# First attention of a macaron network: scores made twice, keys on partitions the second time, mask added by TensorE

## The reference

```python
q = (x @ Wq + bq).reshape(B, S, H, hd).transpose(0, 2, 1, 3)   # B 8, S 512, H 16, hd 8
k, v = ...                                                      # the same with Wk, Wv
scores = einsum('bhqd,bhkd->bhqk', q, k) / sqrt(hd)
band = abs(idx[:, None] - idx[None, :]) <= half                 # half = w // 2, w from 24 to 120
attn = softmax(where(band, scores, -1e30), axis=-1)
out = einsum('bhqk,bhkd->bhqd', attn, v)
out = einsum('bhqd,hdk->bhqk', out, W_o)                        # then @ Wfc + bfc, added to x
```

## Time and profile before

| | |
|---|---|
| median of 3 runs | 3266.82 us (3265.24 to 3267.09) |
| the profiled execution, its own time | 3267.73 us |
| its span, first to last instruction | 3265.8 us |
| busy in the span: TensorE (PE), its weight loads (PEld) | 81%, 56% |
| VectorE (DVE), ScalarE (ACT), GpSimd (POOL) | 74%, 71%, 50% |
| mean granted TensorE clock | 0.849 of 2.4 GHz |

### The profile page before, as it was taken

The page is one execution under the profiler, slowest core; times in us unless marked ns, Lnnn a source line. Parts: engine busy times, 40 slices in busy tenths (PEclk is TensorE's granted clock), DMA queues, the critical chain, the costliest instruction groups (busy, mean ns, idle before and its releaser), DMA issues. The chain is left out here.

```text
span 3265.8 us, 44956 instructions
## 1 busy us (share of the span) xinstructions
PE 2641.5 (81%) x13816; PEld 1818.6 (56%) x13818; DVE 2432.7 (74%) x4559; ACT 2312.6 (71%) x2789; POOL 1636.1 (50%) x1225
## 2 busy tenths in 40 slices
PE   4999958888859999399996587777777877549998
PEld 3877746666648777287774232232332322248887
DVE  5677757777756777688886787877878878378887
ACT  2555547676735555377772999999999999647776
POOL 2676620000026666454443666766767576444444
PEclk9999979898979999699997667676766676679999
DMA  3111100000001111211110000000000000021111
GB/s 111 52 52 39 39 1 2 0 0 0 0 28 52 52 39 39 79 52 40 52 39 0 0 1 1 1 1 1 1 1 1 1 1 1 0 92 52 52 39 51
DMA packets 13576, 86.60 MB, mean 27 GB/s; under 512 B 2176, under 2 KB 4224, under 8 KB 4224
## 3 DMA queue, kind: packets, MB, share of 16 engines
q1 hardware_dynamic: 13440, 84.96, 7.0%
HBM read 82.33 MB, written 2.62 MB: 26 GB/s over the span
## 5 line engine op out<-in xcount | busy, mean ns | idle before, releaser
L1648 POOL TENSOR_TENSOR A_Y<-A_Y,A_U 128x2048 f32<-128x2048 f32 x86 | 390.0, 4556 | 225.4 <-ACT A_U L1691 225.4
L1724 DVE TENSOR_SCALAR A_U<-ps 128x1024 f32<-128x1024 f32 x256 | 309.3, 1218 | 123.2 <-POOL A_Y L1648 59.3
L1730 DVE SCALAR_TENSOR_TENSOR A_U<-ps,A_U 128x1024 f32<-128x1024 f32 x256 | 311.3, 1216 | 55.6 <-PE ps L1860 55.6
L1860 PE MATMUL ps<-A_QT,A_KT 9*128 9x512 f32 x512 | 182.2, 707 | 194.2 <-DVE A_U L1730 160.9
L477 POOL TENSOR_TENSOR F0b_h<-F0b_h,dn 128x512 f32<-128x512 f32 x128 | 212.4, 1663 | 123.5 <-DVE F0b_h L408 123.3
L477 POOL TENSOR_TENSOR F0a_h<-F0a_h,dn 128x512 f32<-128x512 f32 x128 | 212.5, 1664 | 116.3 <-DVE F0a_h L408 116.1
L1860 PEld LDWEIGHTS ps<-A_QT,A_KT 9*128 9x128 f32 x512 | 66.3, 255 | 331.6 <-DVE A_U L1730 241.3
L1648 POOL TENSOR_TENSOR dn<-dn,A_U 128x2048 f32<-128x2048 f32 x42 | 190.3, 4551 | 112.1 <-ACT A_U L1691 112.1
L1691 ACT ACTIVATE A_U<-A_U 128x2048 f32<-128x2048 f32 (+1 forms) x96 | 236.5, 2464 | 0.0
L1832 PE MATMUL ps<-A_Y,A_VA 128*32 128x512 f32 x688 | 227.5, 795 | 5.8 <-DVE A_OT L1630 3.0
L1088 ACT ACTIVATE A_M<-A_M,A_nmax 128x192 f32<-128x192 f32 (+1 forms) x512 | 203.8, 471 | 34.0 <-DVE A_nmax L1203 32.3
(11 more groups left out here) (365 smaller groups left out, 8350.9 us busy)
## 6 DMA issues: line engine op xcount, KB each, us to landing
dn<-weight_rows SPq DMA_DIRECT2D x32, 1024.0 KB, 4.7
F1a_cwb<-weight_rows SPq DMA_DIRECT2D x16, 1024.0 KB, 4.6
F1b_cwb<-weight_rows SPq DMA_DIRECT2D x16, 1024.0 KB, 4.7
dn<-in_down SPq DMA_DIRECT2D x2, 2048.0 KB, 12.3
stage<-in_up SPq DMA_DIRECT2D x1, 2560.0 KB, 9.1
X<-in_x SPq DMA_DIRECT2D x1, 2048.0 KB, 8.2
F1a_h<-in_up SPq DMA_DIRECT2D x1, 2048.0 KB, 7.7
F1b_h<-in_up SPq DMA_DIRECT2D x1, 2048.0 KB, 7.8
```

The lines of the kernel that those rows point to most:

```text
L1648: eng.tensor_tensor(flat(y_slot(m, h)), flat(y_slot(m, h)), flat(Um[:, h % UR]), ALU.add).then_inc(s["t_ready"], 1)
L1724: eng.tensor_scalar(u_step(n), d_pair(n), 0.0, None, ALU.max).then_inc(s["dp_vector"], 1)
L1730: eng.scalar_tensor_tensor(out=u, in0=g_pair(), scalar=CLAMP, in1=u, op0=ALU.min, op1=ALU.mult).then_inc(s["u_ready"], 1)
L1860: last = eng.matmul(ps[:, 4 + b, :], KT[r:r + 9, pair, kt * P:(kt + 1) * P], QT[r:r + 9, pair, :], start=True, stop=True)
```

## The change

It works on the same tiles in another order.

- A chunk still has 16 units, but a unit is now two **halves**: half `h` is one head and two neighbouring tiles, which share one bank (`half_of`, `half_bank`, three banks in turn). TensorE first writes the mask into the bank with a bf16 matmul by the identity (`edge_b`, 512 columns), then adds the two tiles' scores. One VectorE reduction takes the maxima of both tiles and writes them into column 24 of QA.
- The rows of q are turned a second time with these maxima in (`QM`), KA holds -1 in that place. `shifted`, seven units later (`BEHIND`), makes the scores again with keys on partitions, 25 rows, again with a mask matmul first, 448 columns: they come out less their maxima. ScalarE takes the exponential straight from PSUM to PT (`weights`). The transposes of exponentials, their copies and M are gone.
- `outputs`, eight units behind, works on 192 or 256 queries at a time, all in bank 6, and OT holds a group of four heads in place of a tile.
- q and k rows are transposed by groups of four heads (`turn`, 12 groups of four a chunk), one group in each of three of four units, all through bank 3 and copied by ScalarE (`take_turned`).
- GpSimd makes QA, KA and VA and adds the output bias; projections go through bank 7 one after the other at units 5, 6 and 7. QA, VA and OT are doubled. The chunks are written out in pairs (`all_chunks`), and the last seven units of a chunk's second scores run in the next chunk.

The heart of it:

```diff
-                    for t in range(TPC):
-                        for side, src in enumerate((QA, KA)):
-                            for g in range(4):
-                                last = eng.transpose(ps[:, bank_of(t, side), g * P:(g + 1) * P], ...)
-                def scores(n):
-                    t, u = n // 4, n % 4
-                    lo, hi, w0, w1 = window(t)
-                    for r in range(2):
-                        for b in range(2):
-                            g, j = unit_head(u, r, b)
-                            last = eng.matmul(ps[:, 2 * (n % 2) + b, r * WIN + w0:r * WIN + w1],
-                                              QT[32 * j:32 * j + 24, g, t * P:(t + 1) * P],
-                                              KT[32 * j:32 * j + 24, g, lo:hi], start=True, stop=True)
-                def turn(n):
-                    ...
-                                last = eng.transpose(ps[0:k1 - k0, 4 + k, i * P:(i + 1) * P],
-                                                     M[:, n % MR, b, r, k0:k1], ident[:, :])
+                def turn(number, src, g):
+                    eng.wait_ge(s["taken"], number)
+                    for t in range(TPC):
+                        last = eng.transpose(ps[:, TURN, t * P:(t + 1) * P],
+                            src[:, t, 4 * g:4 * g + 4, :].rearrange("p h r -> p (h r)").bitcast(F32), ident[:, :])
+                    last.then_inc(s["qk_tr"], 1)
+                def scores(c, n, first):
+                    for h in (2 * n, 2 * n + 1):
+                        g, t2, j = half_of(h)
+                        if h >= 3:
+                            eng.wait_ge(s["m_ready"], c * HALVES + h - 2)
+                        ...
+                        r = 32 * j
+                        eng.matmul(ps[:, half_bank(h), :], ident_b[:, :], edge_b[:, t2, :], start=True,
+                                   stop=False, skip_group_check=True)
+                        for t in (2 * t2, 2 * t2 + 1):
+                            lo, hi, w0, w1 = window(t)
+                            last = eng.matmul(ps[:, half_bank(h), (t % 2) * WIN + w0:(t % 2) * WIN + w1],
+                                              QT[r:r + 24, g % 2, t * P:(t + 1) * P],
+                                              KT[r:r + 24, g, lo:hi], start=False, stop=True, skip_group_check=True)
+                        last.then_inc(s["sc_done"], 1)
+                def shifted(c, u, taken=None):
+                    g, m2 = u // 4, u // 2 % 2
+                    n = UNITS * c + u
+                    a, b = span(m2)
+                    ...
+                    for i in range(2):
+                        r = 32 * (2 * (u % 2) + i)
+                        eng.wait_ge(s["exp_done"], 2 * n - 1 + i)
+                        eng.matmul(ps[:, 4 + i, a:b], ident_b[:, :], mask_b[:, a:b], start=True, stop=False, ...)
+                        for m in (2 * m2, 2 * m2 + 1):
+                            lo, hi, w0, w1 = window(m)
+                            last = eng.matmul(ps[:, 4 + i, (m % 2) * WIN + w0:(m % 2) * WIN + w1],
+                                              KT[r:r + 25, g, m * P:(m + 1) * P], QM[r:r + 25, g % 2, lo:hi],
+                                              start=False, stop=True, skip_group_check=True)
+                        last.then_inc(s["s2_done"], 1)
-                                last = eng.tensor_tensor_reduce(M[:, n % MR, b, r, w0:w1],
-                                    ps[:, 2 * (n % 2) + b, r * WIN + w0:r * WIN + w1], mask[:, w0:w1],
-                                    -1.0, 3e38, ALU.add, ALU.min, nmax[:, n % MR, b, r:r + 1])
+                            last = eng.tensor_reduce(
+                                QA[:, p, 2 * t2:2 * t2 + 2, 4 * g + j, 3 * HD:3 * HD + 1]...,
+                                ps[:, half_bank(h), :].rearrange("p (t w) -> p t w", t=2), AX.X, ALU.max)
-                                last = eng.activation(m, m, ACT.Exp, scale=-1.0, bias=nmax[:, n % MR, b, r:r + 1])
+                    for i in range(2):
+                        eng.wait_ge(s["s2_done"], 2 * n + i + 1)
+                        eng.wait_ge(s["pv_done"], pair - 1)
+                        eng.activation(PT[:, m2, 2 * (u % 2) + i, a:b], ps[:, 4 + i, a:b],
+                                       ACT.Exp).then_inc(s["exp_done"], 1)
+                            for j in range(4):
+                                last = eng.matmul(ps[32 * j:32 * j + 32, OUT0, lo:hi], VA[:, p, m, 4 * g + j, :],
+                                                  PT[:, m2, j, (m % 2) * WIN + w0:(m % 2) * WIN + w1],
+                                                  start=(m == 0), stop=(m == TPC - 1), skip_group_check=True)
```

More of the change, by code:

```diff
@@ L1051, in _ @@
+                        all_chunks(eng, chunk)
                         norm_gpsimd(eng, s, B)
@@ new lines, in _ @@
+                        all_chunks(eng, chunk)
+                        for n in range(LAST + 1):
+                            if n == 2:
+                                take_turned(2 + TURNED * B, QM[:, 1, :])
+                            if n == 3:
+                                copy_out(B - 1, 1, 2)
+                            if n < BEHIND:
+                                weights(B - 1, n + UNITS - BEHIND)
+                            if n == 2:
+                                norm_scalar(eng, s, B, B - 2, nxt, SPARE)
@@ L1225, in _ @@
[L1225 to L1234 removed]
+                        eng.drain()
@@ new lines, in _ @@
+                        for b in range(2):
+                            eng.tensor_copy(mask_b[:, b * WIN:(b + 1) * WIN], mask[:, :])
+                            for k in range(2):
+                                eng.tensor_copy(edge_b[:, k, b * WIN:(b + 1) * WIN], mask[:, :])
+                        eng.drain()
+                        eng.memset(edge_b[:, 0, 0:HALO], NEG)
+                        eng.memset(edge_b[:, 1, 2 * WIN - HALO:2 * WIN], NEG)
+                        eng.drain().then_inc(step, 1)
@@ new lines, in chunk @@
+                        def chunk(c, p, done):
+                            first = done == 0
+                            for n in range(UNITS):
+                                maxima(c, p, n)
+                                if n == 0:
+                                    norm_stats_vector(eng, s, c, older(c))
+                                if n == 1:
+                                    norm_apply_vector(eng, s, c, older(c))
+                                if n == 4:
+                                    norm_logits_vector(eng, s, c, older(c), nxt, SPARE)
+                                if n == 5:
+                                    take_q(c + 1)
+                                if n == 6:
+                                    take_k(c + 1)
+                                if not first:
+                                    if 8 <= n < 8 + TPC:
+                                        divide(eng, c, n - 8)
+                                    if n == 14:
+                                        residual(eng, c, last_chunk(c))
@@ new lines, in project @@
+                        def project(part):
+                            for t in range(TPC):
+                                last = eng.matmul(ps[:, SPARE, t * P:(t + 1) * P], xa[:, t * P:(t + 1) * P],
+                                                  qkv_w[lay][:, part * D:(part + 1) * D], start=True, stop=True)
+                            last.then_inc(s["pj_done"], 1)
+                        def turn(number, src, g):
+                            eng.wait_ge(s["taken"], number)
+                            for t in range(TPC):
+                                last = eng.transpose(
+                                    ps[:, TURN, t * P:(t + 1) * P],
+                                    src[:, t, 4 * g:4 * g + 4, :].rearrange("p h r -> p (h r)").bitcast(F32),
+                                    ident[:, :])
+                            last.then_inc(s["qk_tr"], 1)
```

536 lines of the change are left out of this document (284 added, 252 removed).

## The result

| | before | the change |
|---|---|---|
| median | 3266.95 us (3265.24 to 3267.30) | 3449.74 us (3383.87 to 3484.99) |
| profiled execution | 3267.73 | 3484.99, span 3483.3 |
| its mean granted clock | 0.849 | 0.816 |

The change makes the kernel **slower**: the comparison gives a ratio of 1.0406, 95% interval 1.0376 to 1.0435, from the executions at 3383.87 and 3415.25 alone; the other two, the profiled one among them, are over 1.5% longer at a lower clock and count as slow. The medians are 5.6% apart. The four executions lie 3% apart, which before they did not, and their order is that of the mean granted clock: 0.846 in the shortest, then 0.837, 0.817 and 0.816.

What follows compares the result with a forecast made beforehand. TensorE was taken to bound the changed attention: 452 head + 53.5 first chunk + 477.4 seven chunks + 19 drain + 20.7 end = 1022.6 us against 943.3, +79, so 3345 us (2.4% slower), range 3250 to 3450.

Steps and rivals of the forecast that it cites:

- The half, 0.74 us: TensorE's mask matmul and two score matmuls, with changes between full array and strip: 0.74 us, over half not streaming.
- The chunk, 68.2 us: TensorE's work in one new chunk if it never waits: 68.2 us, 47.4 of it for 64 halves.
- The rest of the sum: Phase terms beside the seven chunks: first scores near 452, first chunk 53.5, drain 19, end 20.7 us.
- The first chunk and the drain: First chunk without seven units of second scores, 53.5 us; last seven units of them and four outputs alone, 19.
- The other engines: Work a chunk beside TensorE: VectorE 29 us, ScalarE 31 at most, GpSimd 10, with slack.
- Free change-over, 0.15: Rival in each half: mask and scores overlap, loads hidden, no drain; half 0.41, chunk 46.3, time 3170 us; chance 0.15.
- Loads alone hidden: Rival in each half: only weight loads hide, half 0.605 us, time 3276 us; chance 0.07.
- Clock 1.00 in all middle chunks.: Sign to look for: TensorE's granted clock stays at 1.00 (2.4 GHz) in every middle chunk.
- My clock rival: TensorE partly at 1.2 GHz: a quarter of the time adds 109 us, 3455; all of it, 3781; chance 0.07.
- The argument for 1.00: TensorE's new list has a full-array matmul every 0.74 us, said to speak for clock 1.00 throughout.
- tail and norm: TensorE's turns of outputs and back, output projection, norm turn and logits in a chunk: 4.8 us.
- the mildest case of the clock: Mildest lower-clock case for TensorE, which the range to 3450 us took in; the rest of the clock lay outside.

Runs made afterwards that it cites:

- e5: The changed kernel with every score matmul over all 128 rows instead of one head's 24 or 25 (scores wrong): 3189.91 us, ratio 0.9765.
- e6: The changed kernel with 20 extra mask matmuls a chunk in units 4 and 5, beside the norm's logits: 3401.50 us, ratio 1.0419.
- e7: The changed kernel with VectorE taking each half's maxima twice, the extra one into an unread buffer: 3444.05 us.
- e10: The changed kernel itself, unedited, measured again as base for the extra-mask runs: 3467.55 us (3442.99 to 3502.51), ratio 1.0588.
- e8: e3 with ScalarE's two exponentials of a unit ahead of its copies of the turned rows and outputs: 3187.74 us, ratio 0.9759.
- e12: e8 with TensorE waiting for each first-kind bank ahead of its own mask only, not for both: 3181.99 us, ratio 0.9733.
- e3: The changed kernel with all four masks of a unit (two of each kind) issued first, then all eight scores: 3268.33 us, ratio 1.0004.

## Why the prediction was right, and where not

It said slower, and by the mechanism that the runs show. Point by point:

- **The half, 0.74 us**: right, a little high. 0.71 to 0.74 with a 512-column mask, 0.68 to 0.72 with 448. Mask start to first score 0.32 and 0.29 (0.31 said), back 0.18 to 0.23 (0.19 to 0.22 said). The change-over and its loads were 0.33 of the sum; e5 gives 0.29.
- **The chunk, 68.2 us**: right at the full clock. Behind the ramp no period of the changed kernel is wholly at it; 70.3 has some 9 us at 1.2 GHz. e6 has periods of 71.0 and 70.9 with none, and 20 x 0.215 = 4.3 off leaves 66.6. The 1.6 too much is the halves': 64 of them at some 0.717 are 45.9, not 47.4.
- **The rest of the sum**: the first scores start at 451.5, 452 said. The last output copy (1141.36) to the phase's end (1162.6) is 21.2, 20.7 said. The first chunk and the drain were partly at 1.2 GHz, and no run tests their terms alone.
- **The other engines**: VectorE's reduction is 0.69 and ScalarE's exponential 0.54, inside their bounds, and e7 shows VectorE's slack.
- **Free change-over, 0.15**: refuted by e5. **Loads alone hidden**: refuted by the changed kernel's time line, where 0.32 us lie between mask and score.
- **What failed: "Clock 1.00 in all middle chunks."** Of 3449.74 less 3345, 105 us, and 140 in the profiled execution, the forecast has nothing. With the chunk at 66.6 it would be 7 x 1.6 = 11 less still, 3334. The two ends of the four executions price it: their mean clocks give (1 - 0.816) x 2 x 3483 = 1282 us at 1.2 GHz against 1041, 241 us more, for 101 us more time, 0.42 each (the half at both clocks gives 1 - 0.71 / 1.21 = 0.41). The 328 low us of the profiled attention are then 138, and 3334 + 138 = 3472, near its 3485; the ramp and the drain have some 30 low us more. Even the two shorter executions, 3399.6 in the mean, are 55 us over the forecast. My clock rival named this at 0.07 and a quarter of the time; it was nearly half. The argument for 1.00, a full-array matmul every 0.74 us, looked at the middle of a unit. The falls come from the places between. The logits were in the program before, with falls behind them in its trace, and I had summed their length into "tail and norm" without asking what stands around them. The loop's two jumps were in no term of the sum at all: 3.6 us idle, and 130 of the 328 low us begin with them. By the same 0.42 that is an estimate of 58 us; no run tries the kernel without the loop.

That the range held the median, by 0.3 us, is luck: e10's median, 3467.55, is outside, and four of the kernel's eight executions lie above 3480. Its upper end rested on the mildest case of the clock.

The Trainium skill's "TensorE: Matmul & The Clock Gate", in "The mechanism" of its part on packing small matmuls, says that a weight load is pulled ahead of running matmuls when it goes to a group of rows that does not conflict with them, or to the array's background buffer. The trace agrees within one mode: in e8 the loads of four strips did not add up (eight of 0.18 to 0.19 us within 0.31 us), and the mask's load at 562.07 us ran under the transposes ahead of it. Across the change it does not: the score's load began with the score, 0.29 us behind the mask.

```profile
562.46 0.29 PEld L1348 LDWEIGHTS ps<-A_QM,A_KT 25*128 25x128 f32 x2 [0.29 <-issue]
```

On the clock the same page of the Trainium skill, in "Loop structure matters more than you think", makes staying at full clock a matter of the loop nest. Here the trace shows 154 us at 1.2 GHz with TensorE busy 98% of them, so busy time alone did not bring the clock back.

## What to carry to other kernels

Count how often TensorE changes between the full array and a strip of rows, and price each change there and back (0.29 us here) like an instruction. Where masks or biases are added by a matmul, issue several of them, then all the narrow ones in different strips: the same instructions took 0.33 us a half instead of 0.74, and turned a kernel that was 4 to 6% slower into one that is 2.4 to 2.7% faster (e8 and e12). When the order on one engine is regrouped, regroup the queue of the engine that empties its banks too: e3 gained nothing until ScalarE's order followed. Look in the trace for the jumps of a long loop: here they left TensorE idle for 1.5 to 3.3 us each time.

## What I had not expected

- Work that is thrown away kept the clock up: with 20 extra full-array matmuls a chunk beside the logits, none of seven logits brought a fall, with the same 20 elsewhere six of six did. By the medians the first is 66 us faster than e10, the second 12 slower.
- A jump back over the code of two chunks took TensorE's sequencer 3.3 to 3.8 us, where the kernel before took 0.21 for one chunk, and such jumps stand ahead of 130 us at 1.2 GHz. Why it takes so long is not shown.
- The clock stayed at 1.2 GHz for 154 us with TensorE busy 150 of them. Before the change the low stretches of the attention between 480 and 910 us were at most 7 us long.
- One kernel, measured twice, gave ratios of 1.0406 and 1.0588 whose intervals do not meet. With the clock moving this freely, an interval from one group of runs says little of the next; e5, e8 and e12, whose clock holds, spread by 0.2% or less.
- Four matmuls in four strips, of 192 to 256 columns, cost the time of one: eight scores in 0.41 us.
- Still open: what ends a low stretch, and how much the kernel would gain without the loop's jumps. No run here tries either.
